# Plain float32 for the first two layer 0 tiles, halves for the first part of the last layer 2

## The reference

```python
x = x + (x @ W.T + (x @ lora_A[label]) @ lora_B.T * 0.5)           # layer 0, label by batch
# layer 1: eight thresholds; gi = how many of them |x| is not above
q = clip(round(x / d) + zp, 0, 63); x = x + where(gi == 8, 0, (q - zp) * d)   # d, zp chosen by gi
x = x + x @ weight[adapter].T                                      # layer 2, adapter by batch
x = x + (x @ B[adapter].T) @ A[adapter].T                          # layer 3, rank 16
```

## Time and profile before

| | |
|---|---|
| median of 3 runs | 460.23 us (459.65 to 460.66) |
| the profiled execution | 459.77 us, of it a span of 458.0 us |
| PE busy | 446.3 us, 97% |
| DVE busy | 423.1 us, 92% |
| ACT busy | 357.5 us, 78% |
| POOL busy | 34.6 us, 8% |
| granted TensorE clock | 1.000 over the span |

### The profile page before, as it was taken

One profiled execution on the slowest core, in us unless ns is written; L12 is line 12 of the kernel. 1 busy time (PEld: TensorE's weight loads), 2 busy tenths in 40 slices (PEclk: granted clock), 3 DMA queues, 4 the chain that ended last, 5 costly groups with the idle time before them and its releaser, 6 DMA issues.

```text
span 458.0 us, 7875 instructions
## 1 busy us (share of the span) xinstructions
PE 446.3 (97%) x3118; PEld 408.1 (89%) x3118; DVE 423.1 (92%) x409; ACT 357.5 (78%) x330; POOL 34.6 (8%) x46
## 2 busy tenths in 40 slices
PE   7999999999999999999999999999999998999995
PEld 6899999889898999989998999989998998998784
DVE  4889999999899998999899998999969999999983
ACT  5699999987799777977799775997569958676730
POOL 1000011010101000000101000110100101000000
PEclk9999999999999999999999999999999999999999
DMA  7963453596359835687459835486353626378022
GB/s 287 334 241 105 92 135 100 134 224 212 82 167 244 248 89 151 184 220 228 82 180 232 244 92 149 143 215 174 76 188 117 168 63 166 122 212 318 1 92 92
DMA packets 35352, 75.62 MB, mean 165 GB/s; under 512 B 3956, under 2 KB 14068, under 8 KB 34548
## 3 DMA queue, kind: packets, MB, share of 16 engines
q1 hardware_dynamic: 30420, 61.50, 40.3%
q0 software_dynamic: 4896, 13.63, 16.8%
HBM read 53.10 MB, written 8.39 MB: 134 GB/s over the span
## 4 chain that ended last, share of the span: by engine, by line
PE 64%; DVE 23%; issue 8%; DMA 2%; ACT 2%; SPq 1%; DVEq 0%; ACTq 0%
PE l_ps L925 31%; PE l_ps L990 18%; DVE quant L784 8%; DVE cand L758 6%; PE l_ps L1002 5%; PE l_ps L1018 3%; DVE cand L766 2%; DVE x L736 2%; PE bx_ps L951 2%; PE bx_ps L1037 2%; DVE quant L778 1%; DMA a_raw<-a 1%; PE l_ps L935 1%; DVE x L835 1%; DMA adapter_ids<-adapters 1%
## 5 line engine op out<-in xcount | busy, mean ns | idle before, releaser
L990 PE MATMUL l_ps<-x,w_sb 128*128 128x256 f32 x672 | 150.3, 380 | 0.9 <-DVE x L736 0.9
L784 DVE COPY_PREDICATED quant<-mask,cand 128x2048 f32<-128x2048 int8 (+2 forms) x77 | 146.0, 1897 | 0.4
L990 PEld LDWEIGHTS l_ps<-x,w_sb 128*128 128x128 f32 x672 | 125.9, 190 | 19.4 <-issue 2.1
L566 ACT ACTIVATE cand<-x,inv_delta 128x2048 f32<-128x2048 f32 (+2 forms) x88 | 134.4, 1527 | 8.8 <-DVE quant L778 7.0
L576 ACT ACTIVATE mask<-magnitude,thr_bias 128x2048 fp8e5<-128x2048 f32 (+2 forms) x77 | 117.5, 1526 | 9.0 <-DVE quant L784 8.2
L758 DVE TENSOR_SCALAR cand<-cand,delta 128x2048 f32<-128x2048 f32 (+2 forms) x88 | 87.6, 996 | 7.7 <-ACT cand L566 7.4
L766 DVE TENSOR_SCALAR cand<-cand,lower,upper 128x2048 f32<-128x2048 f32 (+2 forms) x88 | 92.8, 1055 | 0.4
L925 PE MATMUL l_ps<-x_hi,w_hi 128*128 128x256 f32 x512 | 86.1, 290 | 1.9 <-ACT w_hi L467 1.0
L925 PE MATMUL l_ps<-x_hi,w_lo 128*128 128x256 f32 x512 | 82.8, 283 | 0.0
L925 PE MATMUL l_ps<-x_lo,w_hi 128*128 128x256 f32 x512 | 82.5, 283 | 0.0
L925 PEld LDWEIGHTS l_ps<-x_hi,w_hi 128*128 128x128 f32 x512 | 71.0, 191 | 7.7 <-issue 4.1
(11 more groups left out here) (84 smaller groups left out, 384.6 us busy)
## 6 DMA issues: line engine op xcount, KB each, us to landing
w_sb<-w SPq DMA_DIRECT2D x60, 384.0 KB, 3.8
out<-x SPq DMA_DIRECT2D x32, 256.0 KB, 2.3
x_raw<-x SPq DMA_DIRECT2D x15, 512.0 KB, 5.9
w_edge<-w SPq DMA_DIRECT2D x28, 256.0 KB, 3.5
w_lo<-w_edge POOLq DMA_DIRECT2D x28, 256.0 KB, 4.7
x_lo<-x_raw POOLq DMA_DIRECT2D x6, 1024.0 KB, 8.6
cand<-w SPq DMA_DIRECT2D x7, 512.0 KB, 7.6
x<-a SPq DMA_DIRECT2D x7, 512.0 KB, 3.4
```

The source lines that it names most:

```text
L566: act.activation(cand[:, c % CANDS, 0:n], x2_unit(u), ACT.Identity, bias=ROUND, scale=inv_delta[:, k:k + 1]).then_inc(rounded, 1)
L784: dve.copy_predicated(y, mask[:, m % MASKS, 0:n].bitcast(I8), t).then_inc(merged, 1)
L990: last = nc.tensor.matmul(l2_bank(b, q)[:, i * S:(i + 1) * S], w2_block(b, o, k), x2[:, b % SLOTS, k * S:(k + 1) * S], start=(i == 0 and k ...
```

## The change

At the start, tiles n = 0 and 1 (o = 0 and 2) of batch 0 are made plain, from the raw weights and the raw `x`, in an order of blocks that follows the loads (`first_tiles`). Their halves are still made, for batches 1 to 7. `x` is loaded in quarters and the first two weight tiles in halves, in a new order; tiles 6 and 7 are staged in `quant`; `WARM` is 10. Tile n = 2 is split in two halves. `x` of batch 1 is split before the first unit instead of inside it. Some closing products (`close0`) of batches 1 and 2 and ScalarE's drains in unit 0 move.

At the end, the last batch's k blocks 0 and 1 of layer 2 are made as halves too, behind the plain blocks 2 and 3 (`last_first_part`). Tiles 0 to 3 are split by ScalarE as two pairs, tiles 4 to 7 one by one, and six GpSimd transfers add the raw values. The halves lie in `x_hi` and `x_lo`. VectorE also splits the last batch's `x2`. Pair 2 of the last batch, like pair 3, gets `x3` added by TensorE (`add_up`) and is copied out by ScalarE. SyncE's queue from batch 1's loading on keeps its order.

```diff
-WARM = 14
+WARM = 10
+ADDED_UP = (3, 2)
...
         def w0_stage(n):
+            if n >= 2 * CANDS:
+                return quant[:, n % 2 * T * P:(n % 2 + 1) * T * P]
...
+        def x2_halves(b):
+            if b == B - 1:
+                return x_hi[:, b % 2, 0:EX], x_lo[:, b % 2, 0:EX]
+            return x2_hi[:, :], x2_lo[:, :]
...
                 sp.dma_start(edge_tile(B - 1, o), w2[bass.ds(adapter, 1), o, :, 0:EW].rearrange("l p w -> p (l w)"))\
-                  .then_inc(last_w2_loaded[o], 16)
+                  .then_inc(last_edge_loaded[o], 16)
...
+            load_first_x(0, x_quarter_loaded[0])
+            load_first_w0(0, 0, w0_half_loaded[0])
+            load_first_x(1, x_loaded[0])
             sp.dma_start(label_ids[:, :], labels.rearrange("(a n) -> a n", a=1)).then_inc(ids_loaded, 16)
             sp.dma_start(adapter_ids[:, :], adapters.rearrange("(a n) -> a n", a=1)).then_inc(ids_loaded, 16)
-            for n in range(1, 5):
-                load_w0(n)
+            load_first_w0(1, 0, w0_half_loaded[1])
+            load_first_x(2, x_quarter_loaded[1])
+            load_first_w0(0, 1, w0_loaded[0])
+            load_first_x(3, x_loaded[1])
+            load_first_w0(1, 1, w0_loaded[1])
+            load_w0(2)
             sp.wait_ge(ids_loaded, 2 * 16)
             load_a0(0)
+            load_w0(3)
             for q in range(4):
                 sp.dma_start(a3_raw(0)[q * QUAD:(q + 1) * QUAD, :], b0).then_inc(b0_loaded, 16)
+            load_w0(4)
             load_w0(5)
...
+                if s == SPLIT:
+                    for q in range(2):
+                        add_last_pair(q)
                 add_edges(s - 1, 3)
...
+            for o in range(RING, T):
+                add_last_edge(o)
...
+            def split_last_pair(q):
+                for o in (2 * q, 2 * q + 1):
+                    act.wait_ge(last_edge_loaded[o], 16)
+                act.wait_ge(l0_done, 2 * (B - 1))
+                hi = last_edges(x_hi, 2 * q, 2)
+                act.activation(hi, x_raw[:, 2 * q * EW:2 * (q + 1) * EW], ACT.Copy).then_inc(w2_hi_done, 1)
+                act.wait_ge(w2_hi_done, 4 * SPLIT + q)
+                act.activation(last_edges(x_lo, 2 * q, 2), hi.bitcast(F32), ACT.Copy, scale=-1.0)\
+                   .then_inc(w2_neg_done, 1)
+
+            def split_last_edge(o):
+                act.wait_ge(last_edge_loaded[o], 16)
+                hi = last_edges(x_hi, o, 1)
+                act.activation(hi, edge_tile(B - 1, o), ACT.Copy).then_inc(w2_hi_done, 1)
+                act.wait_ge(w2_hi_done, 4 * SPLIT + 3 + o - RING)
+                act.activation(last_edges(x_lo, o, 1), hi.bitcast(F32), ACT.Copy, scale=-1.0)\
                    .then_inc(w2_neg_done, 1)
...
                 elif u == LAST:
+                    if j == 1:
+                        split_last_pair(0)
                     if j == 2:
                         split_a3(s - 1)
                     if j == 3:
                         drain_l0(s, 1)
+                    if j == 4:
+                        split_last_pair(1)
                     if j == 5:
                         split_edges(s - 1, 3)
+                elif u == LAST + 1:
+                    if j in (1, 2, 3, 4):
+                        split_last_edge(RING + j - 1)
...
-                if UNITS[u][0] < SPLIT and u > 0:
+                if 0 < u <= LAST:
                     split_x2(UNITS[u][0])
...
+            def first_tiles():
+                pe.wait_ge(x_quarter_loaded[0], 16)
+                pe.wait_ge(w0_half_loaded[0], 16)
+                plain0(0, 1, start=True)
+                plain0(0, 0)
+                pe.wait_ge(x_loaded[0], 16)
+                plain0(0, 2)
+                plain0(0, 3)
+                pe.wait_ge(w0_half_loaded[1], 16)
...
+            def last_first_part():
+
+                b = B - 1
+                pe.wait_ge(x0_done, 2 * B)
+                pe.wait_ge(x2_done, LAST + 1)
+                for o in range(T):
+                    pe.wait_ge(last_w2_loaded[o], 16)
+                    for k in range(EDGE, PARTS[1]):
...
+                pe.wait_ge(x2_split_done, B)
+                x2h, x2l = x2_halves(b)
+                for o in range(T):
+                    if o >= RING:
+                        pe.wait_ge(last_edge_added[o - RING], 16)
+                    elif o % 2 == 0:
+                        pe.wait_ge(w2_added[o // 2], 16 * B)
+                    hi, lo = last_edges(x_hi, o, 1), last_edges(x_lo, o, 1)
+                    for w, v in ((hi, x2h), (hi, x2l), (lo, x2h)):
+                        for k in range(EDGE):
...
             for q in range(4):
                 low_rank3(B - 1, q)
+                if q in ADDED_UP and q < 3:
+                    add_up(q)
+            add_up(3)
```

More of the change, by code:

```diff
@@ L122, in build @@
         x_loaded = [sem(f"x_loaded{h}") for h in range(2)]
-        x_quarter_loaded = sem("x_quarter_loaded")
-        w0_half_loaded = sem("w0_half_loaded")
+        x_quarter_loaded = [sem(f"x_quarter_loaded{h}") for h in range(2)]
+        w0_half_loaded = [sem(f"w0_half_loaded{n}") for n in range(2)]
         a0_loaded = sem("a0_loaded")
@@ L128, in build @@
         last_w2_loaded = [sem(f"last_w2_loaded{o}") for o in range(T)]
+        last_edge_loaded = [sem(f"last_edge_loaded{o}") for o in range(T)]
+        last_edge_added = [sem(f"last_edge_added{o}") for o in range(RING, T)]
         w2_used = sem("w2_used")
@@ L238, in split_pair, with last_edges @@
             return tiles[:, first:first + 2, :]
+        def last_edges(halves, first, n):
+            return halves[:, 0, first * EW:(first + n) * EW]
+        def x2_halves(b):
+            if b == B - 1:
+                return x_hi[:, b % 2, 0:EX], x_lo[:, b % 2, 0:EX]
+            return x2_hi[:, :], x2_lo[:, :]
         def a3_raw(b):
@@ L896, in _ @@
             for q in LAST_ORDER:
-                if q != 3:
+                if q not in ADDED_UP:
                     finish(b, q)
@@ L926, in main0, with plain0 @@
                                              start=(o % 2 == 0 and v is x_hi and w is w0_hi and k == 0), stop=False)
+            def plain0(n, k, start=False):
+                o = ORDER[n]
+                if k == o:
+                    pe.wait_ge(diag_added, n + 1)
+                nc.tensor.matmul(l0_ps[:, 0, o * S:(o + 1) * S], w0_stage(n)[:, k * P:(k + 1) * P],
+                                 x_raw[:, k * S:(k + 1) * S], start=start, stop=False)
+            def first_tiles():
[7 more added lines that the diff above has]
+                pe.wait_ge(w0_half_loaded[1], 16)
+                plain0(1, 0, start=True)
+                plain0(1, 1)
+                plain0(1, 3)
+                plain0(1, 2)
+                pe.wait_ge(w0_loaded[0], 16)
+                pe.wait_ge(x_quarter_loaded[1], 16)
+                plain0(0, 4)
+                plain0(0, 5)
+                pe.wait_ge(x_loaded[1], 16)
+                plain0(0, 6)
+                plain0(0, 7)
+                pe.wait_ge(w0_loaded[1], 16)
+                for k in range(HALF, T):
+                    plain0(1, k)
             def close0(b, o):
@@ L1050, in layer3 @@
                     pe.wait_ge(a3_split_done, b + 1)
-                on_x3 = b == B - 1 and q == 3
+                on_x3 = q in ADDED_UP
                 for i in range(2):
@@ L1056, in layer3, with add_up @@
                 last.then_inc(l3_done, 1)
+            def add_up(q):
+                for i in range(2):
+                    nc.tensor.matmul(l3_bank(B - 1, q)[:, i * S:(i + 1) * S], ident[:, :],
+                                     x3[:, (2 * q + i) * S:(2 * q + i + 1) * S], start=(i == 0), stop=False)
             def layer3_pair(b, q):
@@ L1108, in _ @@
                 low_rank3(B - 1, q)
-            for i in range(2):
-                nc.tensor.matmul(l3_bank(B - 1, 3)[:, i * S:(i + 1) * S], ident[:, :],
-                                 x3[:, (T - 2 + i) * S:(T - 1 + i) * S], start=(i == 0), stop=False)
+                if q in ADDED_UP and q < 3:
+                    add_up(q)
+            add_up(3)
             for q in LAST_ORDER:
```

203 lines of the change are left out of this document (114 added, 89 removed).

## The result

The changed kernel takes 482.12 us (median of 4 runs, 479.96 to 484.44), the kernel before 460.02 on the same chip (459.65 to 460.66). The ratio is 1.048, with a 95% interval of 1.0444 to 1.0518. The forecast was 479.0, with a range of 477.0 to 482.0: the sign and the large term came as forecast, and the size is 3.1 us more, just outside the range. The profiled execution took 483.42 us with a span of 481.5, which is 23.5 us over the span before (458.0). It is one of the two longer ones of the four, so its rows add up to more than the 22.1 us between the medians.

The account below looks back on a forecast made before the run. The bounding chain changes engines: TensorE, VectorE's quantising to 113.86, TensorE to 335.77, mainly VectorE to 435.59, then TensorE. Terms 0.2 + 17.0 + 1.1 + 0.1 + 0.4 = 18.8 on 460.2 gave 479.0 us, range 477.0 to 482.0.

Parts of the forecast that it names:

- the sign: Whole kernel: slower than before, given a chance of 0.97.
- the large term: Last batch's pairs: ScalarE waits for late edge loads, making VectorE's scaling of candidate 3 17.0 us late.
- The stall: Last unit: ScalarE waits for the second edge, VectorE's scaling of candidate 3 comes 17.0 us late, bounds 16.4 and 17.4.
- The start: Batch 0 up to the drain at 113.8: first scaling at 29.3, net +0.2 us, ends -0.6 and +0.8.
- The 0.4 us that the forecast let come back: From 30 to 225 us: VectorE's 0.8 us of waits for candidates can come back, taking +0.6 to +0.2.
- rival A: TensorE's clock falls after idling; behind sum_bx this adds 1.4 us, giving 480.4, the first stretch hidden; chance 0.3.
- split_x2 and the edges: Behind the last unit's update: VectorE's cast and subtraction add 1.1 us, ScalarE's four edge splits 0.1.
- The tail: Very end: add_up(2)'s four passes cost 0.75, with VectorE's lost finish and ScalarE's earlier copy together +0.4 us.
- Less some 0.1 that TensorE had to wait: Tail: the four passes' 0.87 us is reduced by 0.1 that TensorE waited for the last drain anyway.
- The return of 0.35 from ScalarE's second copy: Tail: ScalarE's second copy ends about 0.35 us ahead of where that one did.
- TensorE's saved work: Last batch: 16 plain blocks save TensorE 1.2 us ahead of sum_bx(6), which waits for ScalarE; worth nothing.

Follow-up runs that it names:

- e1: The changed kernel with the loads of the last batch's edges 0 to 3 issued a stage earlier; 466.27 us.
- e3: Only the start of the change, with the end of the kernel before; 462.59 us, ratio 1.0072.
- e6: e3 with nine matmuls of the identity on TensorE ahead of batch 3; 462.19 us, ratio 1.0052.
- e10: e6 with VectorE's add_diag(5) and add_diag(6) put ahead of split_w0(4) and split_w0(5); 460.43 us, ratio 1.0022.
- e5: e3 with b0's loads asked for behind weight tile 4, and the work on b0 moved behind that tile's splits; 461.99 us, ratio 1.0055.
- e2: Only the end of the change, with the start of the kernel before; 480.42 us, ratio 1.0467.
- e7: e2 with e1's edit, edges 0 to 3 loaded a stage earlier; 464.64 us, ratio 1.0111.
- e8: e7 with eleven matmuls of the identity on TensorE ahead of sum_bx(6); 462.95 us, ratio 1.0071.
- e9: e8 with ADDED_UP = (3,), so VectorE finishes quarter 2 of the last batch again; 461.51 us, ratio 1.0046.
- e12: The changed kernel with e1's edit, nine and eleven identity matmuls as fillers, e10's order and ADDED_UP = (3,); 462.13 us, ratio 1.0050.

## Why the prediction was right, and where it was wrong

**The stall (17.0 forecast, 16.25 measured).** This step was right in its mechanism and in every place it named: ScalarE idle 20.97 us in front of the pair's copy, VectorE 16.14 in front of the scaling, TensorE 13.9 in front of its third pair of layer 2. The 0.75 us between are from the second edge, on which ScalarE waits. SyncE issued the first at 408.81, which is 404.08 plus the 4.8 by which everything was late. The second left 0.6 us behind it, not 1.45 as in the trace before, and took 3.5 us to land, so it was there at 412.9, where my 408.9 plus 4.76 would be 413.7. Nothing gave the stall back later, as forecast. e1 shows the cause, since moving the four loads takes the stall away: the change moved the use of the edges by 20 us and left their loads in the queue where they were.

**The start (+0.2 forecast, +3.27 measured): the step that failed.** The prediction says "with weights landing as before, I get 29.3" for VectorE's first scaling, and it came at 32.25. In the new starts it is the first scaling that counts: ScalarE's drain of batch 2 follows it by 84.87 us in e1 (114.53 - 29.66), by 84.88 in the changed kernel (117.13 - 32.25) and by 84.85 in e3, so nothing in the quantising between takes lateness back. The 0.4 us that the forecast let come back did not. Most of the miss of 2.95 us is the landing. The tiles did not land as before: VectorE added tile 4's diagonal at 14.73 before the change, where b0 is asked for behind that tile, and at 20.02 in the changed kernel, where b0 stands ahead of it, after waits of 1.12 and 1.34 us for tiles 3 and 4. It also varies under one and the same queue: the diagonal comes at 17.42 in e1, 18.78 in e3 and 19.05 in e6. With e1's landing the forecast's 29.3 was off by just 0.36, and the drain by 0.67, which is inside the forecast's ends. So part of the 3.27 is this execution's bad luck; the medians of e3's faster pair and of e6, 2.3 and 2.7 us over before, say what the start costs as a rule, still ten times the forecast. The smaller part is the order. It is worth 1.55 us by e10, but I had seen the wait for tile 5 ("about 1 us") and only not the same for the tile behind it (0.64). The two are not independent, since e5 took away the waits for landing and got waits of one engine for the other in their place. From 14 to 18 us, where VectorE waits for tiles 3 and 4, the core's transfers move 188 GB/s with their engines busy, against 408 from 10 to 12. How much of that is b0's doing was not measured by itself and stays open.

**The clock (0 in the sum, rival A at +1.4).** Rival A held as a mechanism. It priced a fall at 1.4 us where TensorE sets the pace, and the falls cost 1.5 to 1.7. It was right too that the long idle stretch around 410 would cost nothing. It had looked for it at one place of two. In the profiled execution the fall came at batch 3 (+1.49), behind a wait of 2.11 us that the prediction had listed and priced at nothing; there was none at `sum_bx(6)`, where the clock stayed at 1.00 after 2.62 us of idle time. In e1 it came at both places, in e2 at the second. It isn't in every execution: e3's pairs of runs are 1.7 us apart, e7's fastest 1.8 to 2.9 us ahead of the other three. A part of the spread of the changed kernel, 479.96 to 484.44 with mean clocks of 0.981 and 0.975, is from this too; its 4.5 us are more than one such fall, and the landing at the start varies as well. The Trainium skill (TensorE: Matmul & The Clock Gate, Part 1) says that TensorE falls back to 1.2 GHz when idle; the rows of 0.50 to 0.60 agree. It says too that the clock's window of observation runs free and is not reset when a kernel starts, so that one kernel can meet a change at different points from run to run. That fits runs of one kernel with and without a fall, though no run here shows that it is the reason.

**split_x2 and the edges (+1.2 forecast, +1.25 measured, +1.7 in e8).** Right. In e8, e7 and e9 VectorE's cast waits 0.46 us more for the update ahead of it. The changed kernel, e1 and e12 have no such wait. The stall does not hide it, since e1 and e12 have no stall; where it comes from stays open.

**The tail (+0.4 forecast, +1.20 measured).** The term was mis-sized. The four passes took 1.06 us and not 0.87. "Less some 0.1 that TensorE had to wait" was wrong in its sign, since splitting one group of low rank products into two around the addition cost 0.14 more. The return of 0.35 from ScalarE's second copy did not come. e9, which undoes both, is 1.4 us faster by the median and 1.21 by its rows.

**TensorE's saved work.** As forecast it is worth nothing. In front of the partial sum TensorE waits 2.62 us for ScalarE in the changed kernel, and in e8 it had room for 22 passes of filler and still waited 1.25. What TensorE does behind batch 0, the low rank sum of batch 1, moved by just 0.76 us (34.74, against 35.50 before) and not by 2.6. `low_rank0(0)` still began 2.2 us earlier (13.31 against 15.50), and 1.04 us went into a wait for VectorE's low rank split on the way; the rest was not followed. As it ends in a wait in front of batch 3, this changed nothing.

**What stays open.** e12 is 2.6 us above before. Its trace places 2.3 us: 0.40 at the drain before the last stages (336.17 against 335.77), 1.45 from there to the copy of the partial sums (100.85 against 99.40), mostly `split_x2`, and 0.41 from that copy to the split of bx (16.41 against 16.00), which is the filler's overrun and not the change's. A smaller filler was not tried. e10 is 0.93 above before by its median; its drain of batch 2 is 0.46 late (114.32 against 113.86) and nothing is added behind it, and the other half is no more than the spread of single executions. No version was found that beats the kernel before.

**The terms together.** By the rows of the profiled execution the start was 3.07 us over its term, the clock 1.49, the split of x2 0.05 and the tail 0.80, and the stall 0.75 under: 4.66 us, which is 23.46 less the 18.8 forecast. That the median came within 3.1 us of the forecast owes something to the stall's opposite error and to two runs with a higher mean clock.

## What to carry to other kernels

When work is moved to an earlier place on one engine, walk to the queue that loads its data: if the load stands behind something that needs the later place, the engine stops, and the whole stall (16 us here) passes on. When work is reordered on two engines that hand pieces to each other, put the small step that releases the partner ahead of the big step of one's own; two such swaps gave 1.6 us back. A new idle stretch of TensorE of 2 to 4 us is not free even where it stands in a wait that was priced at nothing: it can cost 1.5 to 1.7 us behind it, and a few filler matmuls of the right length take that away. The length has to be fitted to each version: twenty cost 2.5 us where nine were right, and the eleven that suited e8 ran 0.5 us over in e9 and e12.

## What the runs showed of the hardware

Idle stretches of 2.11 us (changed kernel, e1), 3.08 (e1) and 3.81 (e2) were followed by a granted clock of 0.50 to 0.66; others of 2.06 us (e3), 1.98 (e7) and 2.62 (changed kernel) were not. The low stretch lasted 3 to 4 us each time. So the length of the idle stretch alone does not tell which way it goes. The same tile, asked for at the same place of the same queue, reached VectorE 2.6 us apart in two executions at the start (17.42 and 20.02), the largest difference between executions that the traces here show and that was not the clock's.
